# One change to a fused four-layer kernel: the state stage's order on four engines, and the root in its tail

## The reference

```
x1 = silu(depthwise_3x3(grouped_1x1(x, w1)))
u, z = split(x1 @ in_proj);   u = silu(causal_conv3(u) + b)
delta = softplus(dt_proj(u @ x_proj[dt]) + b);  B, C = u @ x_proj[B], u @ x_proj[C]
h[t] = exp(delta[t] * A) * h[t-1] + (delta[t] * u[t]) * B[t]       # 8 states per channel
y = sum over states of h[t] * C[t] + u * D;   y = (y * silu(z)) @ out_proj
x1 = (y - mean) * rsqrt(var + 1e-5) * gamma + beta                 # over channels
out = grouped_1x1(x1 * silu(grouped_1x1(x, w2)), wout)
```

## Time and profile before

| what | us |
|---|---|
| median of 3 runs | 485.19 |
| lowest and highest run | 482.53, 485.9 |
| the profiled execution, its own time | 486.84 |
| its span, first to last instruction | 485.1 |
| TensorE, VectorE busy | 352.6 (73%), 368.8 (76%) |
| ScalarE, GpSimd busy | 300.8 (62%), 232.8 (48%) |
| mean granted clock of TensorE | 0.865 |

### The profile page before, as it was taken

One profiled execution on the slowest core, in us unless ns is written; L12 is line 12 of the kernel. 1 busy time (PEld: TensorE's weight loads), 2 busy tenths in 40 slices (PEclk: granted clock), 3 DMA queues, 4 the chain that ended last, 5 costly groups with the idle time before them and its releaser, 6 DMA issues. The chain is left out here.

```text
span 485.1 us, 10561 instructions
## 1 busy us (share of the span) xinstructions
PE 352.6 (73%) x3749; PEld 233.0 (48%) x3749; DVE 368.8 (76%) x682; ACT 300.8 (62%) x582; POOL 232.8 (48%) x220
## 2 busy tenths in 40 slices
PE   4149888895889887977684755675974729988885
PEld 3037666664755342332241212222763318877774
DVE  3799999998895398698869999997645685644443
ACT  3327788877784999398549845435768454343342
POOL 4526868775563507948945995840341350000000
PEclk9567999998899998598978978588885777999999
DMA  6110000000314005022000000000000000111111
GB/s 143 5 18 3 4 0 0 0 1 0 86 30 106 12 2 113 1 47 66 1 1 0 1 0 0 0 1 1 2 1 4 1 0 5 25 19 19 23 19 24
DMA packets 23879, 9.52 MB, mean 20 GB/s; under 512 B 20521, under 2 KB 22313, under 8 KB 23849
## 3 DMA queue, kind: packets, MB, share of 16 engines
q1 hardware_dynamic: 23720, 9.13, 9.4%
q0 software_dynamic: 128, 0.01, 0.2%
HBM read 2.00 MB, written 1.61 MB: 7 GB/s over the span
## 5 line engine op out<-in xcount | busy, mean ns | idle before, releaser
L471 POOL TENSOR_TENSOR Pr<-Pr,rc 128x392 f32<-128x392 f32 x64 | 54.4, 883 | 32.0 <-DVE rc L1786 32.0
L502 POOL TENSOR_TENSOR YA<-YA,hC 128x784 f32<-128x784 f32 x27 | 51.1, 1893 | 31.2 <-DVE hC L1869 30.2
L1329 PE MATMUL pair<-BCf,sel 96*128 96x392 bf16 x128 | 37.8, 397 | 34.5 <-DVE Hs L1853 30.4
L1853 DVE TENSOR_TENSOR_SCAN Hs<-dA,pair 128x784 f32<-128x784 f32 x32 | 57.1, 1785 | 1.7 <-issue 0.7
L1177 PE MATMUL pair<-ident,Pr 128*128 128x128 f32 x256 | 40.8, 291 | 13.2 <-ACT PT L718 8.7
L1329 PEld LDWEIGHTS pair<-BCf,sel 96*128 96x128 bf16 x128 | 10.3, 104 | 70.0 <-issue 65.7
L1177 PEld LDWEIGHTS pair<-ident,Pr 128*128 128x128 f32 x256 | 29.2, 146 | 24.9 <-ACT PT L718 15.8
L1846 DVE TENSOR_TENSOR pair<-DU,pair 128x784 f32<-128x784 f32 x32 | 31.1, 972 | 7.1 <-PE pair L1329 6.3
L718 ACT ACTIVATE PT<-pair 128x392 f32<-128x392 f32 x64 | 31.3, 496 | 5.7 <-PE pair L1177 5.4
L727 ACT ACTIVATE Pr<-Ts 128x392 f32<-128x392 f32 x64 | 32.5, 536 | 3.3 <-DVE Ts L1770 3.3
L1764 DVE TENSOR_REDUCE mx<-pair 128x8 f32<-128x392 f32 x64 | 32.6, 550 | 1.7 <-PE pair L1134 1.5
(11 more groups left out here) (259 smaller groups left out, 936.9 us busy)
## 6 DMA issues: line engine op xcount, KB each, us to landing
SX<-XP SPq DMA_DIRECT2D x48, 112.2 KB
XT<-in_x SPq DMA_DIRECT2D x4, 392.0 KB, 5.7
out<-Os SPq DMA_DIRECT2D x28, 56.0 KB, 1.7
NB<-in_L_conv_x_proj_w SPq DMA_DIRECT2D x4, 3.0 KB
DW<-in_L_conv_dw SPq DMA_DIRECT2D x4, 1.1 KB
vec<-in_L_conv_b_qkv POOLq DMA_DIRECT2D x3, 0.5 KB, 6.3
W<-in_L_conv_w_qkv SPq DMA_DIRECT2D x1, 48.0 KB
BL<-in_L_conv_bi SPq DMA_DIRECT2D x3, 0.5 KB
```

The lines of the kernel that those rows point to most:

```text
L471: eng.tensor_tensor(pg, pg, bcast(rc[:, g, :], 2, WT), ALU.mult).then_inc(pn_r, 1)
L502: eng.tensor_tensor(y, y, hC[:, n % NHC, :], ALU.add).then_inc(g_ya, 1)
L1329: ins = eng.matmul(SPREAD[s][:, columns(h)], sel[:, n, :], upper(BCf[:, c % 2, s, columns(h)]), start=True, stop=True)
L1853: eng.tensor_tensor_scan(Hs[:, n % 2, :], dA[:, n % NA, :], SPREAD[0], 0.0, ALU.mult, ALU.add).then_inc(v_s, 1)
```

## The change

It touches the order of the state stage and the tail, and one operation of the tail.

- `padded(2, 2)` moves from image 0's loop to a place ahead of the first delta; `padded(3, 3)` from the start of image 1 to the end of image 0. `x2(0)` and `gate(0)` change places on TensorE and ScalarE, `x2(1)` comes ahead of `gate(1)`, and `x2(2)` goes to the end of its image's list.
- `conv`, `inner` and `out` of the next and last image are issued in smaller pieces between the spreads.
- `DU` of images 1 to 3 is made by GpSimd, in `delta(k)`, right after delta.
- The decays of the next image are made in two groups, with silus between.
- In the tail, Sqrt and reciprocal become Ln and Exp with scale -0.5, both on ScalarE, with a small Ln ahead of the wait; `scaled` and `gated` go half by half.
- `gate_in(3)` and its two `gate_out` move behind the 14 groups of factors, and its PSUM pair changes.

The diff, with some helpers' parts left out (`conv`, `inner`, `out` and `product` get an argument that says which taps or halves are issued; waits stay with the first, the release with the last):

```diff
@@ -285,7 +286,7 @@
         SPREAD = [pairs[i][:, :, :].rearrange("p h t -> p (h t)")[:, 512 - HT:512 + HT] for i in range(2)]
         FACTORS = (2, 3, 0, 1)
-        GATE_PAIR = (0, 2, 3, 2)
+        GATE_PAIR = (0, 2, 3, 3)
         FINAL = (4, 6, 0, 2)
         def gate_bank(m):
@@ -518,6 +519,10 @@
         if k >= 2:
             eng.wait_ge(a_da, DS * (k - 1))
         eng.tensor_tensor(DL[:, k % 2, :], mk, rest, ALU.subtract).then_inc(v_dl, 1)
+        eng.wait_ge(v_dl, k + 1)
+        if k >= 2:
+            eng.wait_ge(v_b, DS * (k - 1))
+        eng.tensor_tensor(DU[:, k % 2, :], DL[:, k % 2, :], US[:, k, :], ALU.mult).then_inc(v_du, 1)
     def scaled(m):
@@ -868,7 +873,7 @@
     copy_bc(0, 1, "xC")
     sp_w(0)
     gn_exp(2, 3)
-    silu_z(0)
+    silu_x2(0)
     silu_conv(1, 0)
     silu_conv(1, 1)
     decays(0, 0, 1, 2, 3)
@@ -896,7 +901,7 @@
         if i == 0:
             silu_u(1, 0)
             silu_u(1, 1)
-            silu_x2(0)
+            silu_z(0)
             decays(0, 4)
             sp_abs(1, 0)
             sp_abs(1, 1)
@@ -914,11 +919,12 @@
             gn_exp(3, 4)
             silu_conv(2, 0)
             silu_conv(2, 1)
+            silu_x2(1)
+            decays(1, 0, 1)
             silu_u(2, 0)
             silu_z(1)
-            decays(1, 0, 1, 2, 3)
             silu_u(2, 1)
-            silu_x2(1)
+            decays(1, 2, 3)
         elif i == 1:
             sp_abs(2, 0)
             sp_abs(2, 1)
@@ -938,12 +944,13 @@
             var_exp(0)
             decays(1, 7)
             silu_conv(3, 0)
+            silu_conv(3, 1)
             silu_z(2)
-            silu_conv(3, 1)
-            silu_x2(2)
+            decays(2, 0, 1)
             silu_u(3, 0)
             silu_u(3, 1)
-            decays(2, 0, 1, 2, 3)
+            silu_x2(2)
+            decays(2, 2, 3)
         elif i == 2:
             sp_abs(3, 0)
             sp_abs(3, 1)
@@ -1005,6 +1012,8 @@
     image(1)
     turned(0)
     turned(1)
+
+    eng.activation(early_ln[:, :], epsc[:, :], ACT.Ln)
     eng.wait_ge(g_nt0, J - 1)
     eng.wait_ge(p_["var"], J - 1)
     for h in range(2):
@@ -1013,7 +1022,10 @@
         eng.activation(cS[:, columns(h)], tail_result("out", h), ACT.Identity, scale=vec[:, V_GA:V_GA + 1])
     for h in range(2):
         eng.wait_ge(p_["var"], J + h)
-        eng.activation(rs[:, columns(h)], tail_result("var", h), ACT.Sqrt, bias=epsc[:, 0:1]).then_inc(c_["var"], 1)
+        eng.activation(rs[:, columns(h)], tail_result("var", h), ACT.Ln, bias=epsc[:, 0:1]).then_inc(c_["var"], 1)
+    for h in range(2):
+        eng.wait_ge(c_["var"], J + h)
+        eng.activation(rs[:, columns(h)], rs[:, columns(h)], ACT.Exp, scale=-0.5).then_inc(a_rs, 1)
     deviation(2, 3, 5)
     eng.wait_ge(n_nm, 2)
     image(2)
@@ -1031,8 +1043,8 @@
             gate_out(2 + n)
         if n in (3, 4):
             gate_out(1 + n)
-        if n in (9, 10):
-            gate_out(n - 3)
+    gate_out(6)
+    gate_out(7)
     for g in range(G):
         eng.wait_ge(t_z, g + 1)
         take_z(eng, g, (1, 2, 3)).then_inc(t_za, 1)
...
@@ -1315,7 +1331,7 @@
     product("xB", 0, WBC[:, 0, :], US[:, 0, :])
     pe_att(17, 1)
     product("xC", 0, WBC[:, 1, :], US[:, 0, :])
-    gate(0)
+    x2(0)
     conv(1, 0)
     conv(1, 1)
     eng.wait_ge(s_sel, 1)
...
@@ -1363,7 +1379,7 @@
             inner(1, 0)
             inner(1, 1)
             bc("B", 1)
-            x2(0)
+            gate(0)
             delta(1, 0)
             delta(1, 1)
             bc("B", 2)
@@ -1372,22 +1388,25 @@
             bc("B", 3)
             x_c(1)
             bc("C", 2)
-            gate(1)
+            conv(2, 0, (0,))
             bc("B", 4)
-            conv(2, 0, (0, 1))
+            conv(2, 0, (1,))
             bc("C", 3)
+            conv(2, 0, (2,))
             bc("B", 5)
-            conv(2, 0, (2,))
             conv(2, 1, (0,))
             bc("C", 4)
+            conv(2, 1, (1,))
             bc("B", 6)
-            conv(2, 1, (1, 2))
+            conv(2, 1, (2,))
             bc("C", 5)
-            inner(2, 0)
+            x2(1)
             bc("B", 7)
+            inner(2, 0, (0,))
             bc("C", 6)
-            x2(1)
+            inner(2, 0, (1, 2))
             spread(1, "B", 0)
+            gate(1)
             bc("C", 7)
             inner(2, 1)
         elif i == 1:
@@ -1398,29 +1417,34 @@
             bc("C", 0)
             x_c(2)
             bc("B", 2)
+            out(0, (0,))
             bc("C", 1)
-            out(0)
+            out(0, (1,))
             bc("B", 3)
+            conv(3, 0, (0,))
             bc("C", 2)
             var(0)
             bc("B", 4)
-            conv(3, 0, (0, 1))
+            conv(3, 0, (1,))
             bc("C", 3)
+            conv(3, 0, (2,))
             bc("B", 5)
-            conv(3, 0, (2,))
+            conv(3, 1, (0,))
             bc("C", 4)
+            conv(3, 1, (1,))
+            bc("B", 6)
+            conv(3, 1, (2,))
+            bc("C", 5)
             gate(2)
-            bc("B", 6)
-            conv(3, 1, (0, 1))
-            bc("C", 5)
-            conv(3, 1, (2,))
+            bc("B", 7)
+            inner(3, 0, (0,))
+            bc("C", 6)
+            inner(3, 0, (1, 2))
+            spread(2, "B", 0)
+            inner(3, 1, (0, 1))
+            bc("C", 7)
+            inner(3, 1, (2,))
             x2(2)
-            bc("B", 7)
-            inner(3, 0)
-            bc("C", 6)
-            inner(3, 1)
-            spread(2, "B", 0)
-            bc("C", 7)
         elif i == 2:
             delta(3, 0)
             delta(3, 1)
@@ -1522,9 +1546,8 @@
             ins = eng.matmul(bk[:, P * r:P * r + P], (XR0, XR1)[side][:, i].rearrange("p b k -> p (b k)"),
                              BD[:, U_A + side, :], start=True, stop=True)
         ins.then_inc(t_pr, 1)
-        if n == 6:
-            eng.wait_ge(t_gd, 4)
-            gate_in(3)
+    eng.wait_ge(t_gd, 6)
+    gate_in(3)
     eng.wait_ge(t_sg, 14)
     for g in range(G):
@@ -1834,6 +1857,7 @@
     eng.wait_ge(a_w, 1)
     eng.wait_ge(v_cc, 1)
     eng.tensor_tensor(rest, rest, sp[:, SP_U, :], ALU.mult).then_inc(g_cw, 1)
+    padded(2, 2)
     eng.wait_ge(g_ml, 1)
     eng.wait_ge(g_cw, 1)
     eng.tensor_tensor(DL[:, 0, :], mk, rest, ALU.subtract).then_inc(v_dl, 1)
...
@@ -1910,9 +1930,7 @@
         if c == 0:
             times_c(0, 0)
             slot(0, 1)
-            padded(2, 2)
         elif c == 1:
-            padded(3, 3)
             outputs(0)
             slot(1, 1)
             times_c(1, 0)
@@ -1940,21 +1958,17 @@
             column_stats(0)
         slot(c, 5)
         times_c(c, 4)
-        if c == 1:
-            delta_u(2)
-        elif c == 2:
+        if c == 2:
             residual(0)
         elif c == J - 1:
             norm(2)
         slot(c, 6)
         times_c(c, 5)
-        if c == 2:
-            delta_u(3)
         if c < J - 1:
             slot(c, 7)
             times_c(c, 6)
             if c == 0:
-                delta_u(1)
+                padded(3, 3)
             times_b(c + 1, 0)
             times_c(c, 7)
         else:
@@ -1995,10 +2009,6 @@
     eng.wait_ge(p_["wout"], J - 1)
     eng.wait_ge(c_["x2"], J)
-    def inverse_root(h):
-        eng.wait_ge(c_["var"], J + h)
-        eng.reciprocal(rs[:, columns(h)], rs[:, columns(h)]).then_inc(a_rs, 1)
-
     def scaled(h):
         eng.wait_ge(a_rs, J + h)
         eng.tensor_tensor(nt[:, columns(h)], cS[:, columns(h)], rs[:, columns(h)], ALU.mult).then_inc(v_n0, 1)
@@ -2008,14 +2018,12 @@
         eng.scalar_tensor_tensor(nt[:, columns(h)], nt[:, columns(h)], vec[:, V_BE:V_BE + 1], X2[:, J - 1, columns(h)],
                                  ALU.add, ALU.mult).then_inc(v_nt, 1)
-    inverse_root(0)
-    inverse_root(1)
     scaled(0)
+    gated(0)
+    scaled(1)
+    gated(1)
     inverse(2, 3, 2)
-    scaled(1)
     minus_mean(2, 3)
-    gated(0)
-    gated(1)
     for h in range(2):
         xs = X[:, (J - 1) * T + HT * h:(J - 1) * T + HT * h + HT]
         eng.wait_ge(p_["wout"], J + h)
```

32 lines of the change are left out of this document (17 added, 15 removed).

## The result

| | before | after |
|---|---|---|
| median of 20 runs each, us | 484.98 | 483.76 |
| lowest and highest | 480.37, 487.03 | 477.19, 486.56 |
| profiled execution, own time | 486.84 | 480.16 |
| its span | 485.1 | 477.6 |

A forecast was written before the change was run, and what follows sets the result against it. VectorE was taken as the bound, its path broken by a dozen us of waits. Terms -0.7 - 5.8 - 1.3 - 3.8 - 1.3 = -12.9 took the profiled 486.84 us to 473.9, said as a median of 472.5, range 469 to 476.

The forecast's parts named there:

- the 2.09 us wait: TensorE's wait for the third image's strips ahead of its convolution; early strips were to remove it.
- First image, -0.7: First image's state stage: GpSimd's own work fixes its end; -0.7 us, between -1.3 and +1.5.
- The wall: outputs(0) waits for all seven GpSimd adds of its image, forecast to end at 198.61 + 14.7 = 213.3.
- Second image, -5.8 (bound -2): Stretch outputs(0) to outputs(1): 41.8 us becomes 36.0, set by GpSimd; -5.8 us, ends -8.2 and -2.
- Third image, -1.3: Third image's state stage: delta-u (1.05 us) and a small wait go; -1.3 us, between 0 and -2.
- Fourth image, 0: Fourth image's state stage: same order, 0, and 1.5 us either way by GpSimd's adds against VectorE's products.
- Tail, -3.8: After the state stage: Ln and Exp by halves start the factors earlier; -3.8 us, between -4.1 and -2.6.
- rival 4: Tail: Ln and Exp share a table, no load between them, 1.28 us less; 471.2 us, chance 0.02.
- Last gate, -1.3: End of the tail: gate_in(3) moves from between the factors into TensorE's 2.2 us wait; -1.3 us, bounds 0 and -1.3.
- Rival 1: State stage: GpSimd is the bound in all three images; -8.0 us, 477.2 us, chance 0.23.
- Rival 2: TensorE at 1.2 GHz through the convolutions: 491.8 us, chance 0.03; through the convolution alone: 478, chance 0.12.
- Rival 5: State stage: early strips put the spreads' wait in the DMA's place, pieces change nothing; 479 us, chance 0.04.

The follow-up runs named there:

- early_pad: du_pool with padded(2, 2) early and x2(0) and gate(0) exchanged, nothing else of the new order; 475.53 us, ratio 0.9808.
- late_claim: The changed kernel with each piece of the convolution one spread later, in both images; 481.16 us, ratio 0.9897.
- gate_back: late_claim with the second image's gate product back between C of state 2 and B of state 4, its silu first on ScalarE; 477.04 us, ratio 0.9846.
- again: The changed kernel once more, unaltered; 484.37 us, ratio 0.9926 to the kernel before.
- state_only: The changed kernel with the old tail; 486.82 us, ratio 1.0055 to the kernel before.
- du_dve: The changed kernel with delta-u back on VectorE at its old places; 483.62 us, ratio 0.9941.
- late_weights: The changed kernel with GpSimd's later_weights put behind the add (3, 1); 484.75 us, ratio 0.9955.
- before2: The kernel before once more, for a second profile; 483.92 us in one run.
- tail_only: The kernel before with the new tail alone (Ln, Exp, scaled and gated by halves, the last gate); 479.11 us, ratio 0.9883.
- best: du_pool with GpSimd's add of the skip term held back until VectorE's second product of outputs(2) is done; 473.70 us, ratio 0.9772.
- du_pool: tail_only with delta-u moved to GpSimd, in the old order of the state stage; 476.55 us, ratio 0.9831.
- du_pool2: The same kernel as du_pool, run and profiled again; 474.90 us, ratio 0.9808.
- warm: late_claim with ten unused float32 products in TensorE's pause ahead of conv(2, 0); 476.97 us, ratio 0.9854.
- warm_only: The changed kernel with ten unused products in its pause, pieces of convolution unchanged; 478.03 us, ratio 0.9869.
- tail_warm: tail_only with ten unused products in the pause, in place of the gate product, which goes behind the next spread; 478.69 us, ratio 0.9855.

## Why the prediction was wrong

**The step that failed** is the one of the third image: "Its 12 strip transfers, on SP's queue, start some 9 us earlier, nothing else is on that queue, and the 2.09 us wait goes." The transfers did start early, and the wait stayed. The convolution has two conditions, the strips and its PSUM pair, and the earlier trace rows name the one that came last. The other, the copy of `xC(1)`, ended at 188.75 + 0.80 = 189.55 in the kernel before, 0.36 us ahead of the convolution's start at 189.91. I asked of the released wait only what had released it, not what would be next; that row of ScalarE stood in the trace:

```profile
188.75 0.80 ACT L818 ACTIVATE BCf<-pair 96x784 f32<-96x784 f32 x1
```

`early_pad` shows it directly: with the strips early the pause is still 1.50 us, its releaser is the copy, and the convolution starts 0.2 us sooner, not the 2.09 that I took the strips to be worth.

With it go three things that the sum had at nothing.
- *The piece stands ahead of a spread.* The pieces were costed by their length, 0.8 or 1.42 us, not by the claim that the first of them carries. VectorE waited 2.04 and 2.14 us behind it in the two images. The first of these waits cost little, as GpSimd's adds held `outputs(0)` (below), and in the second image the variance product, 2.62 us at a clock that was low for nearly all of it, stands between the claim and the spread as well. What `late_claim` gives back is 3.2 us by the medians, 1.4 by the ratios.
- *The gate product is gone from the pause.* I counted it as moved at no cost. It had filled 1.5 us of TensorE's wait for that copy; without it the pause is 3.41 us. What the move costs by itself no run shows, since `gate_back` moves ScalarE's silu of z too.
- *The clock.* In all five profiles with 3.4 us between C of state 2 and the first piece (after, `again`, `state_only`, `du_dve`, `late_weights`; not six, as I wrote ahead of `gate_back`) the granted clock falls to 0.50 between 186.8 and 188.8 us. It is back at about 201 in after and `state_only` and at 204 to 206 in the other three; the second image takes 37.7 and 37.5 us in the first two, 40.2 and 40.3 in `again` and `late_weights`. With the 2.05 to 2.10 us of the old order it fell in four (before, `before2`, `tail_only`, `best`) and stayed at 1.00 in two (`du_pool`, `du_pool2`). With 1.5 us it fell in two (`gate_back`, and `late_claim`, which had idled 1.40 before as well) and stayed in one (`early_pad`). With the unused products it stayed in four of four. So the pause decides in part; what tells the cases of the middle apart is open.

**What the clock costs** shows at one place: ScalarE's second silu of the convolution. From the first milestone it comes after 28.6 to 28.9 us at full clock in the old order, 31.6 to 32.1 at half; in the new it is 29.5 and 29.8 at full clock (`warm`, `warm_only`) and 32.9 to 33.4 at half. So the fallen clock makes it some 3 us late in either order (2.7 to 3.9). GpSimd can start its next image only 17 to 19 us after that silu, when ScalarE has gone through u, z, the decays and the softplus. At full clock (`du_pool2`) it starts

```profile
212.56 2.43 POOL L507 TENSOR_TENSOR sp<-sp 128x784 f32<-128x784 f32 x1 [1.35 <-ACT sp L882]
```

1.3 us after `outputs(0)`, and the second image takes 36.3 us; in the two profiles of the changed kernel it starts 6.4 and 7.2 after, and takes 37.7 and 40.2.

**Point by point.**
- *First image, -0.7*: measured -0.13 and +0.40 for `padded(2)`, which was not covered. In the new order GpSimd's adds set `outputs(0)`, at half clock and at full: they end at 203.05 + 7.97 = 211.02 in after, 0.04 us ahead of it, and in `warm`, at full clock, VectorE comes early and waits, and the image takes 39.99 us where after has 40.03:

```profile
210.98 1.03 DVE L1915 SCALAR_TENSOR_TENSOR yz<-US,vec,YA 128x784 f32<-128x784 f32 x1 [5.58 <-POOL YA L503]
```

  The wall itself was right, closer than its terms deserve: from delta's start I had 14.7 us, and 196.31 to 211.02 is 14.71. The collision of `padded(3)` is in the four adds, 7.97 where four of 1.84 would be 7.36, so 0.6. The fault was to put the gain on the distance between milestones while delta itself stayed where ScalarE sets it.
- *Second image, -5.8 (bound -2)*: -1.4, outside the bound. Of the 4.4 us between, 2.0 are the 41.8 that I subtracted from: one execution's, where the mean of three is 39.8. The other 2.4 are the new order's 38.4, where I had 36.0. I took GpSimd's own work as 29.9 us plus 0.7; in the profile of after it runs from 217.46 to 247.96, 30.5. What failed is its start, which I held at 5.45 us or earlier: it is 6.3 to 7.2 us. VectorE then stands beside GpSimd's last adds with `nt`, 2.38 us, and `outputs(1)` starts 0.76 us after the last add. In `late_claim` it is the adds that `outputs(1)` waits for:

```profile
251.29 1.03 DVE L1908 SCALAR_TENSOR_TENSOR yz<-US,vec,YA 128x784 f32<-128x784 f32 x1 [1.75 <-POOL YA L503]
```

  In `du_pool2` the second image takes 36.3 us, near the forecast of 36.0, but by luck: with its start at +1.3 my sum has GpSimd done at +31.9, and its adds end at +35.5.
- *Third image, -1.3*: +0.6. Delta-u went, and the norm beside GpSimd took its place: `nt` is 5.8 us for three in the groups above, 2.4 each in the second and the third image. The two table loads were covered as said: ScalarE still waits for TensorE's u between them. But VectorE reached `outputs(1)` earlier and ScalarE's softplus did not come earlier with it: GpSimd's remainder starts 254.19 - 248.72 = 5.5 us after it, where it was 4.2 before.
- *Fourth image, 0*: +2.1. GpSimd is later against VectorE, and so meets it at the worst place. GpSimd and VectorE of after:

```profile
286.95 2.54 POOL L554 TENSOR_TENSOR BD<-W,bd 128x1408 f32<-128x1408 f32 x1
289.45 2.56 POOL L539 TENSOR_TENSOR YA<-YA,S 128x784 f32<-128x784 f32 x1
```
```profile
287.12 3.20 DVE L1908 SCALAR_TENSOR_TENSOR yz<-US,vec,YA 128x784 f32<-128x784 f32 x1
290.35 2.49 DVE L1911 TENSOR_TENSOR yz<-yz,ZS 128x784 f32<-128x784 f32 x1
```

  VectorE's 3.20 us were 1.03 before, which is the +2.1; the 2.49 were there before as well. Each ends 0.83 us behind the GpSimd instruction beside it. The Trainium skill, "SBUF — State Buffer", section "SBUF: two separate sides", has a rule for it: the port pair that the two engines share is an exclusive lock, and when a VectorE instruction with two inputs in SBUF meets a GpSimd one, the first to start has it for its whole length and the other blocks. The rows agree with it. The price of such a collision is then about what is left of GpSimd's instruction (289.49 - 287.12 = 2.4 us here, for 3.20 - 1.03 = 2.2 us more), not the fixed 0.7 that I took.
- *Tail, -3.8*: from scan (3, 7) to VectorE's product of the first group of factors it took 18.9 us in after, 20.1 in `again`, 19.7 in `tail_only`, against 22.25 and 22.5 in before and `before2`, so -2.1 to -3.6, a little under the forecast. The half of `wout` took 0.93 us, between my two cases, in after; in `tail_only` all of `wout` took 2.88, at half clock.
- *Two loads, not one set*: there is a load of 1.28 us between Ln and Exp, so rival 4 is out. The Trainium skill, "ScalarE: Activation LUTs", section "What ACT_TABLE_LOAD costs", has 2.66 us with a drain; in this trace the instruction behind follows at once:

```profile
326.78 1.25 ACT L1025 ACTIVATE rs<-pair,epsc 128x392 f32<-128x392 f32 x2
328.05 1.28 ACT L1028 ACT_TABLE_LOAD   x1
329.35 0.95 ACT L1028 ACTIVATE rs<-rs 128x392 f32<-128x392 f32 x2
```

- *Last gate, -1.3*: from the first to the last of VectorE's 14 products of the factors 11.62 us against 12.93, -1.31.

**The rivals.** None was it alone. Rival 1 (477.2, chance 0.23) had the bound right for the first two images: GpSimd's adds set `outputs(0)` and nearly `outputs(1)`, and ScalarE sets when GpSimd starts. In the third they don't; there the adds end at 285.32, 1.8 us ahead of `outputs(2)`. It had neither the later start nor the fourth image, and its second image, -4, was counted from the same 41.8. Rival 2, at its half-way size (478, chance 0.12), named the right effect, with its pause at another place (ahead of B of state 5), and let the early strips and the order gain the rest; the strips gained 0.2 us (`early_pad`), and the state stage as a whole lost. Rival 5 (479, 0.04) named the first mechanism, a wait of another name in the place of the DMA's, and put it at the spreads rather than the claim. These came together, and with the fourth image the time is above my range. Of the signs I named, `outputs(1)` near 249 came true (248.72) and meant nothing: this execution had reached the state stage 2.9 us earlier. The wait ahead of `outputs(0)` for GpSimd's add came (0.29 us). The sign that told of the miss was the sum of VectorE's waits for spreads in the two stretches: I wanted under 5 us, and they are 0.69 + 2.04 + 0.80 + 0.80 + 0.83 and 0.73 + 0.68 + 2.14 + 0.61, 9.3. It is no measure of the time, though: `late_claim` has 10.8.

**Open** is why the clock stays up after some pauses of 1.5 to 2.1 us and falls after others, and how much of the 6 us (3.7 by the ratios) between the changed kernel and `warm_only` is the clock alone in an order where ScalarE is not late as well: `gate_back` is 477.04 with the clock at half in its profile, `warm` 476.97 with it full.

## What to carry to other kernels

A wait that a trace names is the last of several: before a step removes it, look for the next one in the same instruction, here the reader of the PSUM buffer it claims, and put down the difference (0.36 us), not the wait (2.09). A product that starts with a claim costs what stands behind it the claim's wait, however short the product is. A wait on one engine is a loss only if nothing later holds the same step: here GpSimd's adds hid VectorE's waits in the first image. Work that is moved out of a pause lengthens the pause, and a longer pause may cost the clock of what follows. Before a sum subtracts from a stretch, read that stretch in more than one profile (41.75 us in one here, 38.84 in the next), and compare distances between milestones, not the time at which one of them came.

## What the runs showed of the hardware that I had not expected

- In the changed kernel's profile the granted clock is 0.50, 1.2 GHz, from 187.3 to 200.9 us, though TensorE is busy 14.00 of the 14.00 us from 187 to 201, with pieces of the convolution (96 by 32 products of 392 columns) and spreads. At the next block products (199.69, 2.11 us for four records that take 1.59 in `early_pad` at full clock) it comes up; in `again` it is still at half through them (200.25, 2.81 us for four) and comes up at about 204. So 14 us of unbroken work did not bring it back. Whether the shape of the products has to do with it, no run tells.
- Ten products without a use, 2.39 us, ahead of the convolution kept it at 1.00 in four profiles of four. They paid 4 to 6 us by the medians (2.1 to 3.7 by the ratios) in the new order, and nothing that can be told in the old one (478.69 and 476.43 against 479.11 and 474.90 to 476.55).
- The times of the changed kernel spread over 9.4 us in 20 runs (477.19 to 486.56), those of `warm_only` over 4.1 and of `warm` over 2.8 in six each. The filled pause is not shown to be the cause: `gate_back`, whose clock fell in its profile, spreads over 2.5 us, and `tail_warm`, where it stayed up, over 5.5.
